# Feature sums of the last layer norm: from GpSimd and TensorE to VectorE and ScalarE

## The reference

```python
x = _layernorm(x + _L0_attn_ref(x, ...), axis=-1)     # linear attention, 32 heads of 128, gated
x = _layernorm(x + _L0_xattn_ref(x, ctx, ...), axis=-1)  # fake-quantised product with a context
x = _layernorm(x + _L0_ffn_ref(x, up, down, perm), axis=-1)

def _layernorm(x, axis=-1, eps=1e-05):
    m = jnp.mean(x, axis=axis, keepdims=True)
    v = jnp.var(x, axis=axis, keepdims=True)
    return (x - m) / jnp.sqrt(v + eps)

# _L0_ffn_ref: 16 groups of 64 permuted features, each 64 -> 256 -> 64
t = x.reshape(b * l, Dm)[:, perm].reshape(b * l, h, d)
t = jax.nn.gelu(jnp.einsum('bhd,hdm->bhm', t, up), approximate=False)
t = jnp.einsum('bhm,hmd->bhd', t, down).reshape(b * l, h * d)[:, unperm]
```

## Time and profile before

| | us |
|---|---|
| median of 3 runs | 1976.04 (1975.78 to 1977.31) |
| profiled execution, own time | 1974.85 |
| its span | 1973.0 |
| TensorE busy | 1868.7 (95%) |
| VectorE busy | 1293.2 (66%) |
| ScalarE busy | 869.1 (44%) |
| GpSimd busy | 505.4 (26%) |

### The profile page before, as it was taken

How to read it: one execution, slowest core, us unless ns; L and a number is a source line. 1 busy time by engine, 2 the same in 40 slices (tenths; PEclk the granted TensorE clock), 3 DMA queues, 4 the chain that set the end, 5 groups by cost and what they waited for, 6 DMA issues and landing times.

```text
span 1973.0 us, 25499 instructions
## 1 busy us (share of the span) xinstructions
PE 1868.7 (95%) x9397; PEld 893.9 (45%) x9397; DVE 1293.2 (66%) x1794; ACT 869.1 (44%) x1278; POOL 505.4 (26%) x414
## 2 busy tenths in 40 slices
PE   7999999999999999999999999999999999967895
PEld 5344444444444444444444444444444444734321
DVE  7676766766676767667665757576666667557633
ACT  5453544444344535444443435353444445324652
POOL 3232122221322321222222223222122223012354
PEclk9999999999999999999999999999999999978998
DMA  4112222221312322222212112121212222242311
GB/s 183 43 64 86 65 87 64 101 71 67 99 50 91 81 86 65 88 63 101 71 67 68 49 59 81 54 74 66 50 69 65 75 65 75 58 135 80 98 53 70
DMA packets 117786, 149.59 MB, mean 76 GB/s; under 512 B 67232, under 2 KB 83744, under 8 KB 117280
## 3 DMA queue, kind: packets, MB, share of 16 engines
q1 hardware_dynamic: 106208, 135.29, 22.3%
q0 software_dynamic: 2560, 8.39, 1.3%
q10 hardware_dynamic: 8896, 4.28, 0.8%
HBM read 119.63 MB, written 12.58 MB: 67 GB/s over the span
## 4 chain that ended last, share of the span: by engine, by line
PE 74%; DVE 8%; DMA 5%; ACT 5%; issue 4%; POOL 3%; SPq 1%; ACTq 0%; POOLq 0%; DVEq 0%
PE bank L1090 18%; PE bank L1117 15%; PE bank L1119 15%; PE bank L1118 15%; ACT w_pair L1265 2%; DMA v_split<-w_vo 2%; DVE w_pair L1385 2%; DMA raw_pair<-w_vt 2%; PE bank L1159 2%; PE bank L1160 2%; PE bank L1161 2%; PE bank L1235 1%; PE bank L1227 1%; POOL raw_pair L1596 1%; DVE bank L1440 1%
## 5 line engine op out<-in xcount | busy, mean ns | idle before, releaser
L1117 PE MATMUL bank<-x_blocks,w_pair 128*128 128x512 f16 (+1 forms) x1820 | 678.9, 373 | 14.9 <-DVE bank L1428 7.7
L1118 PE MATMUL bank<-x_blocks,w_pair 128*128 128x512 f16 (+1 forms) x1820 | 678.6, 373 | 0.0
L1119 PE MATMUL bank<-x_blocks,w_pair 128*128 128x512 f16 (+1 forms) x1820 | 678.4, 373 | 0.0
L1090 PE MATMUL bank<-w_vo,gated_split 128*128 128x512 f16 x1440 | 333.7, 382 | 3.5 <-DVE scores_split L1385 3.5
L1595 POOL TENSOR_TENSOR sums_pair<-raw_pair 128x512 f32<-128x512 f32 x63 | 88.2, 1400 | 851.4 <-DVE w_pair L1385 640.5
L1117 PEld LDWEIGHTS bank<-x_blocks,w_pair 128*128 128x128 f16 x1820 | 178.2, 98 | 219.3 <-DVE bank L1428 16.7
L1119 PEld LDWEIGHTS bank<-x_blocks,w_pair 128*128 128x128 f16 x1820 | 178.3, 98 | 203.3 <-issue 0.8
L1118 PEld LDWEIGHTS bank<-x_blocks,w_pair 128*128 128x128 f16 x1820 | 178.3, 98 | 192.2 <-issue 0.6
L1090 PEld LDWEIGHTS bank<-w_vo,gated_split 128*128 128x128 f16 x1440 | 141.7, 99 | 175.3 <-DVE scores_split L1385 4.4
L1385 DVE SCALAR_TENSOR_TENSOR w_pair<-raw_pair,w_pair 128x1024 f16<-128x1024 f32 x126 | 177.4, 1408 | 48.3 <-ACT w_pair L1265 48.3
L1604 POOL TENSOR_TENSOR ssq<-ssq,sig 128x512 f32<-128x512 f32 x64 | 83.0, 1296 | 455.8 <-ACT sig L1319 455.8
(11 more groups left out here) (175 smaller groups left out, 2120.6 us busy)
## 6 DMA issues: line engine op xcount, KB each, us to landing
raw_pair<-w_qk SPq DMA_DIRECT2D x32, 1024.0 KB, 5.0
raw_pair<-w_gate SPq DMA_DIRECT2D x16, 1024.0 KB, 4.9
raw_pair<-w_out SPq DMA_DIRECT2D x16, 1024.0 KB, 5.0
raw_pair<-w_vt SPq DMA_DIRECT2D x15, 1024.0 KB, 4.9
decay_sb<-decay SPq DMA_DIRECT2D x32, 256.0 KB, 5.2
raw_pair<-ctx_in SPq DMA_DIRECT2D x8, 1024.0 KB, 5.0
acc<-x_t SPq DMA_DIRECT2D x4, 1024.0 KB, 11.5
ctx<-raw_pair SPq DMA_DIRECT2D x8, 512.0 KB, 2.8
```

What stands on the lines that cost most here:

```text
L1090: last = pe.matmul(out, a, b, start=m == 1, stop=m == n)
L1117: pe.matmul(out, w_hi, x_hi, start=unmet and k == 0, stop=False, skip_group_check=halves or not fresh)
L1118: pe.matmul(out, w_hi, x_lo, start=False, stop=False, skip_group_check=halves or not fresh)
L1119: mm = pe.matmul(out, w_lo, x_hi, start=False, stop=k == QT - 1, skip_group_check=halves or not fresh)
```

## The change

`POOL_SUMS`, its steps `sums_first` and `sums` on GpSimd, and the helper buffer are gone. The squares of all 8 tiles are made by ScalarE: that of tile 0 straight into the running sum of squares, the others into the two buffers in turn. VectorE adds each tile to the running sum of values (L1563 of the new kernel), and its square to the running sum of squares (L1566): for batch 0 all tiles, for batch 1 tiles 0 to 6. TensorE does one `total` for a batch, after the last tile: the two running sums (L1237, L1240), and for batch 1 then also tile 7 and its square (L1244, L1246). The two PSUM banks of the totals are taken at that point, and not at tile 1. In batch 0, both semaphore counts of the totals come with the second matmul.

```diff
         def add_sums():
-            if not to_sum:
-                return
-            p, y = to_sum.pop(0)
-            free = self.sum_free[b]
...
+            if to_add and to_add[0][0] < FP - b:
+                p, i, y, sq = to_add.pop(0)
+                if p == 0:
+                    begun.append(sq)
+                else:
+                    self.add("sums", b=b, p=p, i=i, y=y, free=self.sum_free[b][0], sq=sq,
+                             before=begun[0] if p == 1 else self.sum_free[b][1])
+                    self.sum_free[b] = [self.tick("sum1"), self.tick("sum2")]
+                    self.sq_last_free[i] = self.sum_free[b][1]
...
         for n in range(2 * FP + LAG):
...
             self.all_up[b] = n >= 2 * FP
-            add_sums()
+            square()
             if n >= LAG:
                 down_half((n - LAG) // 2, (n - LAG) % 2)
-                total()
+                add_sums()
                 yield
+        square()
         add_sums()
         total()
...
         elif kind == "total":
-            y, sq, first = c.x2p[b][:, st["p"], :], c.decay_sb[st["i"]][:, :], st["first"]
             tot1, tot2 = (c.banks[i][:, :] for i in st["banks"])
+            last = st["last"]
             until(pe, sem, st["free"][0])
+            until(pe, sem, st["sums"][0])
+            pe.matmul(tot1, c.ones32[:, :], c.sums[b][0], start=True, stop=not last)
             until(pe, sem, st["free"][1])
...
+            until(pe, sem, st["sums"][1])
+            mm = pe.matmul(tot2, c.ones32[:, :], c.sums[b][1], start=True, stop=not last)
+            if last:
+                p, i, y, sq = last
+                pe.wait_ge(sem["y"], y[1])
+                pe.matmul(tot1, c.ones32[:, :], c.x2p[b][:, p, :], start=False, stop=True).then_inc(sem["total_mm"])
+                pe.wait_ge(sem["sq_last"], sq[1])
+                pe.matmul(tot2, c.ones32[:, :], c.decay_sb[i][:, :], start=False, stop=True).then_inc(sem["total_mm"])
+            else:
+                mm.then_inc(sem["total_mm"], 2)
...
+        elif kind == "sums":
+            p, (sum1, sum2) = st["p"], c.sums[b]
+            y = c.x2p[b]
+            dve.wait_ge(sem["y"], st["y"][1])
+            until(dve, sem, st["free"])
+            dve.tensor_tensor(sum1, y[:, 0, :] if p == 1 else sum1, y[:, p, :], ALU.add).then_inc(sem["sum1"])
+            dve.wait_ge(sem["sq_last"], st["sq"][1])
+            until(dve, sem, st["before"])
+            dve.tensor_tensor(sum2, sum2, c.decay_sb[st["i"]][:, :], ALU.add).then_inc(sem["sum2"])
...
-        elif kind == "sums":
-            y, (sum1, sum2) = c.x2p[b][:, st["p"], :], c.sums[b]
-            pool.wait_ge(sem["y"], st["y"][1])
-            until(pool, sem, st["sq_free"])
-            pool.tensor_tensor(c.sq32[:, :], y, y, ALU.mult).then_inc(sem["sq_pool"])
-            until(pool, sem, st["free1"])
-            pool.tensor_tensor(sum1, sum1, y, ALU.add).then_inc(sem["sum1"])
-            pool.wait_ge(sem["sq_pool"], st["sq"][1])
-            until(pool, sem, st["free2"])
-            pool.tensor_tensor(sum2, sum2, c.sq32[:, :], ALU.add).then_inc(sem["sum2"])
```

More of the change, by code:

```diff
@@ L33 @@
 NH = 8
-POOL_SUMS = (0, 2, 4)
 QT = KT // 2
@@ L57 @@
      "resid", "stats", "aggr", "var_eps", "rstd", "shift", "normed", "q1_scaled", "q1_clamped", "q1_n", "q1_tmm",
-     "q1_t", "rsum_mm", "rsum", "rowed", "x_mm", "x_acc", "t_mm", "t_copy", "ffn_in", "up_mm", "gelu", "down_mm", "y", "sum_act", "sum1", "sq_pool", "sum2", "sq_last", "total_mm", "mean", "mean2", "var", "var_c",
+     "q1_t", "rsum_mm", "rsum", "rowed", "x_mm", "x_acc", "t_mm", "t_copy", "ffn_in", "up_mm", "gelu", "down_mm", "y", "sum_act", "sum1", "sum2", "sq_last", "total_mm", "mean", "mean2", "var", "var_c",
      "inv", "rs", "y_sub", "y_pool", "y_mul", "stored", "bits_set", "x_t1", "x_t3", "x_t2", "x_t4", "pair_sum",
@@ L122, in __init__ @@
         self.sq_last_free = [None, None]
-        self.sqf_free = None
         self.all_up = [False, False]
@@ L490, in ffn_phase @@
         got, hs, ys, t_y = {}, {}, {}, {}
-        to_sum, to_total, totals, done = [], [], [], []
+        to_sum, to_add, begun, totals, done = [], [], [], [], []
         for p in range(FP):
@@ L524, in down_half @@
                 to_sum.append((p, y))
-        def add_sums():
-            if not to_sum:
-                return
-            p, y = to_sum.pop(0)
-            free = self.sum_free[b]
[L531 to L541, removed]
@@ L543, in total, with square @@
-        def total():
[L544 to L551, removed]
+        def square():
+            if to_sum:
+                p, y = to_sum.pop(0)
+                i = p % 2
+                self.add("square", b=b, p=p, i=i, y=y, free=self.sum_free[b][1] if p == 0 else self.sq_last_free[i])
+                to_add.append((p, i, y, self.tick("sum_act" if p == 0 else "sq_last")))
@@ L552, in total @@
+        def total():
+            totals.extend(self.ring.take() for _ in range(2))
+            st = self.add("total", b=b, banks=[t[1] for t in totals], free=[t[2] for t in totals], sums=list(self.sum_free[b]),
+                          last=to_add.pop(0) if to_add else None)
             done[:] = self.tick("total_mm"), self.tick("total_mm")
-            self.sq_last_free[i] = done[1]
+            if st["last"]:
+                self.sq_last_free[st["last"][1]] = done[1]
         for n in range(2 * FP + LAG):
@@ L843, in final_part @@
     plan.sq_last_free[:] = plan.decay_free
-    plan.sqf_free = plan.s7_free
     plan.h_free[:] = [max(plan.v_hl_free)] * 4 + [plan.g_free[0]] * 2 + [plan.g_free[1]] * 2
@@ L917, in __init__ @@
         self.raw.append(self.sums_pair[:, 0:2].rearrange("p c m -> p (c m)"))
-        self.sq32 = self.s7
         q_flat = self.units["q"][:, :, :, :, :].rearrange("p h n b s -> p (h n b s)")
@@ L1358, in scalar_program @@
                 act.activation(c.hid[st["slots"][a]], c.banks[st["banks"][a]][:, :], ACT.Gelu).then_inc(sem["gelu"])
[L1359 to L1362, removed]
         elif kind == "square":
+            dst = c.sums[b][1] if st["p"] == 0 else c.decay_sb[st["i"]][:, :]
             act.wait_ge(sem["y"], st["y"][1])
             until(act, sem, st["free"])
-            act.activation(c.decay_sb[st["i"]][:, :], c.x2p[b][:, st["p"], :], ACT.Square).then_inc(sem["sq_last"])
+            act.activation(dst, c.x2p[b][:, st["p"], :], ACT.Square).then_inc(sem["sum_act" if st["p"] == 0 else "sq_last"])
         elif kind == "last_stats":
@@ L1623, in gpsimd_program @@
                                     ).then_inc(sem[f"gathered{b}_{p}"], 16)
-        elif kind == "sums_first":
-            pool.wait_ge(sem["y"], st["y"][1])
-            until(pool, sem, st["free1"])
-            pool.tensor_copy(c.sums[b][0], c.x2p[b][:, st["p"], :]).then_inc(sem["sum1"])
-        elif kind == "sums":
-            y, (sum1, sum2) = c.x2p[b][:, st["p"], :], c.sums[b]
-            pool.wait_ge(sem["y"], st["y"][1])
-            until(pool, sem, st["sq_free"])
-            pool.tensor_tensor(c.sq32[:, :], y, y, ALU.mult).then_inc(sem["sq_pool"])
-            until(pool, sem, st["free1"])
-            pool.tensor_tensor(sum1, sum1, y, ALU.add).then_inc(sem["sum1"])
-            pool.wait_ge(sem["sq_pool"], st["sq"][1])
-            until(pool, sem, st["free2"])
-            pool.tensor_tensor(sum2, sum2, c.sq32[:, :], ALU.add).then_inc(sem["sum2"])
         elif kind == "last_shift":
```

## The result

| | before | after |
|---|---|---|
| median of the runs, us | 1975.91 (4 runs, 1975.14 to 1977.31) | 1962.19 (4 runs, 1960.38 to 1963.55) |
| ratio, 95% interval | | 0.9929 [0.9912, 0.9946] |
| profiled execution, its span | 1973.0 | 1961.6 |

13.7 us faster, where 15.3 was forecast. Two repetitions beside other kernels gave 1964.32 against 1976.11 and 1962.79 against 1975.03, so 11.8 and 12.2 us: the gain is 12 to 14 us.

A forecast was written before the change was run, and what follows sets the result against it. TensorE was taken to bound both feature stages, with the totals on its chain; 7.65 + 0.15 - 0.70 + 7.65 + 0.30 + 0.45 - 0.24 = 15.3 us less, from 1976.04 to 1960.7, range 1958.3 to 1964.5.

The forecast's parts named there:

- Batch 0's feature stage: TensorE's chain in batch 0: four totals removed save 7.65 us, a down pair right behind another 0.15; VectorE's adds hidden.
- statistics: Batch 0 after its last tile: the mean waits for the sums and both counts, so 0.70 us is lost.
- Batch 1's feature stage: TensorE stays the bound: four totals save 7.65 us, two closer down pairs 0.30, a wait beside batch 0's scaling 0.45.
- the likeliest case: The whole kernel: 15.3 us less, to 1960.7, with the granted clock at 1.00 between 1895 and 1935; chance 0.68.
- rival 1: TensorE's clock falls in batch 0's statistics: about 3.3 us at half clock cost 1.65 us, so 1962.3; chance 0.14.
- one earlier fall: Around 1861.8 to 1864.8, TensorE idle for 3 us, then at 0.50 of full clock for 3 us; cited for rival 1.
- A stretch with 0.36 us of work in 2.6: From 1836.4 to 1839.0 TensorE was busy for only 0.36 us and stayed at full clock; cited against rival 1.
- Rival 3: VectorE late in batch 1: slow adds of tile 1 delay tile 2's y, TensorE waits 2.4 us, so 1963.1; chance 0.10.
- the meeting that the prediction priced at 1.27: VectorE's add beside batch 0's scaling might take longer by a whole GpSimd subtraction, 1.27 us; y still in time, counted 0.
- Rival 2: Half clock lasts through batch 1's feature stage: 24.3 us of pairs take 48.6, 9 us slower, 1985; chance 0.03.
- rival 4: Something other than TensorE sets batch 1's pace: only batch 0's 7.1 us gained, 1969, or none, 1976; chance 0.05.
- Batch 1's end: After batch 1's last down pair: VectorE's late adds start the mean 3.05 us after it, against 2.81; 0.24 lost.

The follow-up runs named there:

- the wait filled: Changed kernel with up matmuls repeated in TensorE's two waits of batch 0's statistics: 1961.91 us (0.9930 of before).
- two experiments: Changed kernel with batch 0's mean counted with its own total, 1960.39 us; changed kernel with batch 0 done as batch 1, 1960.37 us.
- the adds doubled: Changed kernel with two more dependent VectorE adds behind each tile's two adds, 13 tiles: 1965.88 us (0.9947 of before).
- the matmul three times: Changed kernel with batch 0's mean counted with its own total and the first up matmul of batch 1's half 5 issued three times: 1958.17 us.
- the padded kernels: Changed kernel with up pairs of halves 8 to 15 issued twice, in batch 0 (1969.97 us) or in batch 1 (1969.65 us).

## Why the prediction was right, and where not

**Batch 0's feature stage** and **statistics**: right. 4 totals and a closer down pair, less 0.70 for the late mean: 7.1 forecast, 7.0, 6.8 and 6.9 in the three profiles. In the change's profile TensorE waited 0.6 us for the add of the values and 0.8 for that of the squares. VectorE's adds took 0.69 and lay where they were put:

```profile
1877.13 0.69 DVE L1557 TENSOR_TENSOR acc<-bank,acc 128x512 f32<-128x512 f32 x1 [0.79 <-PE bank L1230]
...
1877.85 0.69 DVE L1563 TENSOR_TENSOR sig<-sig,acc 128x512 f32<-128x512 f32 x1
...
1879.11 0.63 ACT L1361 ACTIVATE decay_sb<-acc 128x512 f32<-128x512 f32 x1
1879.78 0.69 DVE L1566 TENSOR_TENSOR sig<-sig,decay_sb 128x512 f32<-128x512 f32 x1 [1.23 <-ACT decay_sb L1361]
```

y, add, 1.23 us of waiting for the square, add; the next y at 1881.26.

**Batch 1's feature stage**: the mechanism was right, and its forecast of 24.3 us was met as soon as the clock was held (the wait filled). What failed is the assumption in the likeliest case that the clock stays, which had 0.68, against 0.14 for rival 1. I had laid the fall down at 3.3 us of half clock from one earlier fall; it was 6.8, so its price is 3.3 us and not 1.65. That one was not the only fall in the trace before the change. The one ahead of it, at a wait of 4.52 us, lasted about 6.8 us, twice as long, with TensorE at work in the second half of it (the timeline; then stretches with the granted clock):

```profile
1820.65 1.97 PE L1219 MATMUL bank<-ident,acc 128*128 128x128 f32 x8 [4.52 <-ACT acc L1331]
```

```profile
1817.00:1818.00 1.00, 0.00 (x0) 0.00 (x0) 0.97 (x3) 0.00 (x0) 0.00 (x0) 0.82 0.33 100
...
1824.00:1825.00 1.00, 1.00 (x5) 0.43 (x4) 0.00 (x0) 0.97 (x2) 0.00 (x0) 0.77 0.76 230
```

From both lengths, rival 1 would have had a price between 1.65 and 3.4 us. That the median of 1962.2 is what rival 1 gave (1962.3) is no proof of its size, and in part luck: the repetitions say 11.8 and 12.2 us, which is 15.3 less 3.3. Priced in full, rival 1 gives 1964.0, near the upper end of the range, and one repetition had 1964.32. The sum of the likeliest case, 15.3 us, was not the gain of any median of the changed kernel (13.7, 11.8 and 12.2).

The evidence that I set against rival 1 was weak for a reason that can be seen in the rows. A stretch with 0.36 us of work in 2.6 had kept full clock, and I took it as speaking for a stay. The rows do not line up by the length of a wait or by the work beside it: a wait of 1.37 us was followed by full clock before the change; one of 1.39 us, alone or behind one of 0.45, by 3.4 us of half clock in two experiments, and alone by 6.8 in a third (the adds doubled); two waits with 1.09 us of work between by 6.8 in every profile of the changed kernel. What sorts these cases I can't say from the runs. With rows that can't be sorted, a place with two new waits called for a higher chance of a fall than 0.14. The Trainium skill's page TensorE: Matmul & The Clock Gate, Part 1, has the slow clock as the default and activity as what releases it. The trace agrees: with TensorE idle for 1.30 and 1.39 us the clock fell to 0.50, and with these waits filled by repeated matmuls, but for 0.44 us, it stayed at 1.00.

**Rival 3**, VectorE late: not so, but nearer than the median shows. VectorE in the experiment with the matmul three times, beside batch 0's scaling (start us, us):

```profile
1914.23 2.20 DVE L1569 TENSOR_TENSOR gate_units<-acc 128x512 f32<-128x512 f32 x1
1916.36 0.68 DVE L1572 TENSOR_TENSOR gate_units<-gate_units,decay_sb 128x512 f32<-128x512 f32 x1
1916.96 0.68 DVE L1592 TENSOR_TENSOR acc<-acc,sig 128x512 f32<-128x512 f32 x1
1917.56 0.68 DVE L1563 TENSOR_TENSOR acc<-bank,acc 128x512 f32<-128x512 f32 x1
```

The add of tile 1 took 2.20 us in place of 0.69, with a subtraction of GpSimd (1914.59, 1.28 us) inside it. The excess of 1.5 fits the meeting that the prediction priced at 1.27, though by the records VectorE's add had begun first. Tile 2's y ended at 1918.24, and TensorE's up pair that needs its bank began at 1918.65. 0.4 us were left; forecast were 0.65, or 0.2 with one such meeting.

**Rival 2** (half clock through batch 1) and **rival 4** (a hidden gain) are out: full clock came back after 6.8 us in the changed kernel, and no stretch around batch 0's statistics was longer in any experiment; the padded kernels showed 6.8 and 6.9 of the 6.9 us put in. (The trace before the change also has 24 us at half clock, 1742 to 1766, but TensorE had work for only 7.5 of them.) **Batch 1's end**: 0.24 lost was forecast; the wait for the add is there (0.24 us ahead of the first total), and the two means stand as computed once the clock holds.

## What to carry to other kernels

When work is taken off the engine that sets the pace, look at what that engine does in the next wait: on TensorE a wait of 1.3 or 1.4 us, harmless before the change, can take the clock down, and the stretch behind it can cost more than the wait (3.3 us here). Price it as half of the slow stretch, take the length from every fall that the trace has (3.4 and 6.8 us here), and test it by repeating a matmul that overwrites its own result. Where a sum over partitions takes in several tiles and TensorE sets the pace, it was cheaper to add the tiles up on a VectorE with time to spare (0.69 us an add, hidden) than to give each tile its own matmuls with ones (1.91 us for the two of a tile, on the chain); one matmul with ones for each sum is left at the end; and a count that stands for two results makes the reader of the first one wait for both, so look for the buffer that forces it.

## What was not expected of the hardware

The stretch from batch 1's mean to the end, which no kernel here changes, took 22.8 us in most profiles and 21.1 in three of them. The scatters on GpSimd make the difference. The third of them, in the changed kernel's profile and in its repetition, each with VectorE's scalings beside it:

```profile
1952.51 0.74 DVE L1586 TENSOR_TENSOR acc<-acc,gate_units 128x512 f32<-128x512 f32 x1
1952.53 0.96 POOL L1636 DMA_INDIRECT out_t<-acc,perm_sb  x1 [0.30 <-issue]
```

```profile
1950.07 0.69 DVE L1581 TENSOR_TENSOR acc<-acc,gate_units 128x512 f32<-128x512 f32 x1
1950.08 1.51 POOL L1636 DMA_INDIRECT out_t<-acc,perm_sb  x1 [0.30 <-issue]
```

In one the scatter takes 0.96 us and VectorE's operation 0.74, in the other 1.51 and 0.69. Three scatters are slow or fast together, 0.54 us each, so 1.6 in all. The same program takes either way in different executions (one profile had the first slow and the next two fast). I have not tried what decides it; it may be a part of the spread of 3 us between runs of one kernel, which no profile of those runs shows.
